# Two routed feed-forward passes and a recurrence on one core: another order for the router's front, the weights and the scatters

## The reference

```python
x = L0_attn_h
x = x + 0.5 * ffn(layernorm(x))          # first pass
x = x + recurrence(layernorm(x))         # 3 layers of width 64, a scan over each sequence
x = x + 0.5 * ffn(layernorm(x))          # second pass

def ffn(x):                              # 8 experts, the best one of each token
    p = softmax(x @ Wr + br); gate = max(p); e = argmax(p)
    xn = layernorm(x) * ln_g + ln_b
    return (relu(xn @ W1[e] + b1[e]) @ W2[e] + b2[e]) * gate
```

## Time and profile before

| | us |
|---|---|
| median of 3 runs | 731.2 |
| lowest and highest | 726.25, 731.56 |
| the profiled execution | 730.1 |
| its span in the trace | 728.4 |
| PE busy | 667.5 (92%) |
| DVE busy | 409.2 (56%) |
| ACT busy | 270.0 (37%) |
| POOL busy | 173.6 (24%) |

### The profile page before, as it was taken

How to read it: one execution, slowest core, us unless ns; L and a number is a source line. 1 busy time by engine, 2 the same in 40 slices (tenths; PEclk the granted TensorE clock), 3 DMA queues, 4 the chain that set the end, 5 groups by cost and what they waited for, 6 DMA issues and landing times.

```text
span 728.4 us, 15522 instructions
## 1 busy us (share of the span) xinstructions
PE 667.5 (92%) x4414; PEld 583.2 (80%) x4414; DVE 409.2 (56%) x1427; ACT 270.0 (37%) x640; POOL 173.6 (24%) x178
## 2 busy tenths in 40 slices
PE   5567998899999999999998999999899989999993
PEld 4346997699997987888867877878789979999992
DVE  7256676233345667686888677787756533333331
ACT  3222321132325467553553556744422313222220
POOL 4611533211112111113412241123304411111111
PEclk9997999899999999999999999999989999999998
DMA  9929893675654454434615417343274564553540
GB/s 289 288 95 320 270 313 118 232 241 170 205 208 139 154 194 139 146 109 142 234 53 186 145 55 278 133 130 119 68 262 150 200 207 162 189 161 123 168 141 14
DMA packets 59919, 126.51 MB, mean 174 GB/s; under 512 B 8105, under 2 KB 36660, under 8 KB 59700
## 3 DMA queue, kind: packets, MB, share of 16 engines
q1 hardware_dynamic: 53204, 108.50, 44.6%
q0 software_dynamic: 6624, 16.92, 6.4%
HBM read 106.36 MB, written 20.35 MB: 174 GB/s over the span
## 4 chain that ended last, share of the span: by engine, by line
PE 64%; DVE 15%; issue 8%; DVEq 6%; another core or an unknown queue 2%; DMA 2%; ACT 1%; POOL 0%; SPq 0%; POOLq 0%; ACTq 0%
PE bank L1670 27%; PE bank L1684 27%; PE bank L1657 2%; DMA pay<-routed_rows 2%; DVEq L397 2%; DVE st L735 1%; PE bank L1516 1%; PE bank L1578 1%; DVE rec L1070 1%; DVE y_b L1169 1%; DVE act_t L1160 1%; PE bank L1611 1%; PE bank L1585 1%; DVE rec L1046 1%
## 5 line engine op out<-in xcount | busy, mean ns | idle before, releaser
L1670 PE MATMUL bank<-mn_t,w 128*128 128x128 f32 x2368 | 287.0, 278 | 0.1
L1670 PEld LDWEIGHTS bank<-mn_t,w 128*128 128x128 f32 x2368 | 277.4, 194 | 8.2 <-issue 8.0
L1684 PE MATMUL bank<-w,act_t 128*128 x1184 | 277.6, 385 | 5.7 <-DVE res L1175 4.0
L1684 PEld LDWEIGHTS bank<-w,act_t 128*128 128x128 f32 x1184 | 220.2, 192 | 43.5 <-issue 16.7
L1397 ACT ACTIVATE mn_t<-bank,vec 128x128 f32<-128x128 f32 x152 | 61.4, 454 | 228.9 <-PE bank L1657 208.4
L1160 DVE TENSOR_SCALAR act_t<-bank,vec 128x128 f32<-128x128 f32 x296 | 83.4, 344 | 109.1 <-PE bank L1670 94.8
L1407 ACT ACTIVATE act_t<-bank,vec 128x128 f32<-128x128 f32 x296 | 84.7, 368 | 78.0 <-PE bank L1670 75.9
L1169 DVE TENSOR_TENSOR y_b<-bank,b_all 128x256 f32<-128x256 f32 x74 | 31.4, 425 | 110.1 <-PE bank L1684 95.4
L634 POOL DMA_INDIRECT out_x<-res,pay x37 | 37.4, 1011 | 210.5 <-DVE res L1175 131.0
L634 POOL DMA_INDIRECT x_middle<-res,pay x37 | 37.0, 999 | 212.3 <-DVE res L1175 177.6
L625 POOL DMA_INDIRECT routed_rows<-rows,dest x64 | 65.7, 1027 | 64.5 <-DVE dest L840 32.4
(11 more groups left out here) (213 smaller groups left out, 462.2 us busy)
## 6 DMA issues: line engine op xcount, KB each, us to landing
w<-in_L_ffn_W SPq DMA_DIRECT2D x82, 1024.0 KB, 8.7
pay<-routed_rows SPq DMA_DIRECT2D x78, 130.0 KB, 2.1
rows<-in_L_attn_h SPq DMA_DIRECT2D x8, 512.0 KB, 5.5
rows<-x_middle SPq DMA_DIRECT2D x8, 512.0 KB, 4.5
routed_rows<-fill SPq DMA_DIRECT2D x2, 1040.0 KB
routed_rows<-rows,dest POOLq DMA_INDIRECT x64
b_all<-in_L_ffn_b SPq DMA_DIRECT2D x1, 1024.0 KB, 9.0
x_middle<-res,pay POOLq DMA_INDIRECT x37, 2.7
```

The lines of the kernel that those rows point to most:

```text
L1670: last = t.matmul(b_hid[half][:, c % 4 * P:(c % 4 + 1) * P], w1[i % W1S][:, k * F + c * P:k * F + (c + 1) * P], mn_t[p][i % 2][:, k * P:(k ...
L1684: last = t.matmul(b_out[i % 2], act_t[i % 2][:, c * P:(c + 1) * P], w2[:, ds(eb * (WE // FC) + c * D, D)], start=c == 0, stop=c == FC - 1)
```

## The change

- **Constants.** POOL makes the identity first and raises `s_c1` to 1; tri and the counters follow (2), the rest last (3). PE starts at 1, DVE's copies at 2.
- **PE.** It begins with seven unread products (`in_motion(7)`), and waits for `s_c2` only ahead of `router_sums`. Chunk 1's transposes and logits now stand ahead of chunk 0's ranks; `parameters` ahead of chunk 2's turned logits. Chunk 3's transposes, logits and turned logits leave the front for columns 0, 48, 192 and 216, which are slots 0 and 1. ACT's copies follow.
- **DVE.** choose 0, place 0, choose 1, copy of count 0, place 1, copy of count 1. `order_of_use` is gone.
- **POOL.** It issues four scatters, then waits until both counts are copied, then issues twelve.
- **SP.** Chunk 0, router weights, chunk 1, router bias, chunk 2, four second weights, parameters, the other four second weights, chunk 3; after the tables the first weights of slot 0, the rows of slots 0 to 3, the first weights of slot 1, output bias, first weights of slot 2. No weights by use; the first second product waits for all eight.
- **Columns.** The parameters' columns and the log of the sigmoid move from slot 6 (312 of 48 each) to slot 1 (72). Chunk 3 of the recurrence and of the second router moves back by up to some two slots, chunks 0 to 2 hardly.

```diff
-LN_MOMENTS = [[984, 985], [1272, 1273], [1680, 1681], [2064, 2066]]
+LN_MOMENTS = [[984, 985], [1272, 1273], [1680, 1683], [2064, 2113]]
...
-UP = [[5760, 5856], [7057, 7104], [9480, 9504], [10584, 10944]]
+UP = [[5760, 5856], [7057, 7104], [9528, 9600], [11112, 11184]]
...
-CONVOLVE = [[1033, 1300, 1752, 2136], [1176, 1442, 2040, 2352], [1298, 1657, 2256, 2497]]
-GATES = [[4248, 5328, 7056, 8640], [4800, 5832, 8256, 9481], [5208, 6720, 9120, 10176]]
+CONVOLVE = [[1033, 1300, 1752, 2211], [1176, 1442, 2040, 2378], [1298, 1656, 2256, 2616]]
+GATES = [[4248, 5328, 7056, 9048], [4800, 5832, 8256, 9552], [5232, 6721, 9144, 10560]]
...
-R_RANKS = [[None, None, 192, 552], [6240, 7944, 9816, 11280]]
+R_RANKS = [[None, None, 193, 552], [6240, 7944, 9936, 11472]]
...
+R1_TRANSPOSE = [0, 48]
+R1_KEEP = [0, 24]
+R1_LOGITS = 192
+R1_KEEP_LOGITS = 49
+R_TURN_LOGITS = [[None, None, None, 216], [5952, 7368, 9696, 11256]]
 R_SCATTER = [[[None, None, None, None], [None, None, None, None], [72, 120, 168, 216], [264, 312, 360, 408]],
-    [[1560, 1608, 1656, 1704], [2040, 2088, 2136, 2160], [2472, 2520, 2568, 2616], [2808, 2856, 2904, 2952]]]
+    [[1560, 1608, 1656, 1704], [2040, 2088, 2136, 2160], [2472, 2520, 2568, 2616], [2856, 2904, 2952, 3000]]]
...
-LAYER_COLUMNS = 96
-EXP_LOG_A = 120
-LOG_SIGMOID = 312
+LAYER_COLUMNS = 49
+EXP_LOG_A = 72
+LOG_SIGMOID = 72
...
             sp.dma_start(rb_all[:, :], router_b[None, :].to_broadcast([P, E])).then_inc(s_rb, 16)
-            for e in range(EAGER):
+            load_x(0, 2)
+            for e in range(E // 2):
                 second_weights(e)
-            load_x(0, 2)
+            load_parameters()
+            for e in range(E // 2, E):
+                second_weights(e)
             load_x(0, 3)
-            load_parameters()
 
             sp.wait_ge(s_tab, 1)
-            for i in range(2):
-                slot_weights(0, i)
-            sp.wait_ge(s_order, 1)
-            second_weights_by_use(0)
+            slot_weights(0, 0)
             for i in range(RING - 1):
                 next_rows(0, i)
-            second_weights_by_use(1)
+            slot_weights(0, 1)
...
             g.memset(ident[:, :], 0.0)
+            pool.drain()
+            g.affine_select(out=ident[:, :], in_=ident[:, :], compare_op=ALU.not_equal, fill=1.0, base=0,
+                            pattern=[[-1, P]], channel_multiplier=1).then_inc(s_c1, 1)
...
                 for part in range(NJ // 2):
+                    if (c, part) == (0, 2):
+
+                        pool.wait_ge(s_kept[R1], HC)
                     route(0, c, part)
...
-            for c in range(HC):
-                choose(0, c)
-                place(0, c)
-                keep_counts(0, c)
+            choose(0, 0)
+            place(0, 0)
+            choose(0, 1)
+            keep_counts(0, 0)
+            place(0, 1)
+            keep_counts(0, 1)
             for part in range(5):
                 tables(0, 0, part)
-            order_of_use()
...
             def second_expert(p, i):
-                if p == 0 and i < LATER:
-
-                    if i == 0:
-                        pe.wait_ge(s_w, 16 * EAGER)
-                    pe.wait_ge(s_wl[i], 16)
+                if (p, i) == (0, 0):
+                    pe.wait_ge(s_w, 16 * E)
                 return expert_of(pe, p, i)
...
-            pe.wait_ge(s_c2, 1)
+            pe.wait_ge(s_c1, 1)
+            in_motion(7)
             for part in range(2):
                 transposes(R1, 0, part)
+            pe.wait_ge(s_c2, 1)
             router_sums()
             pe.wait_ge(s_wrk, 1)
             logits(R1, 0)
+            transposes(R1, 1, 0)
             turn_logits(0, 0)
-            transposes(R1, 1, 0)
-            ranks(0, 0)
             transposes(R1, 1, 1)
             logits(R1, 1)
+            ranks(0, 0)
             turn_logits(0, 1)
             counts(0, 0)
+            ranks(0, 1)
             transposes(R1, 2, 0)
-            ranks(0, 1)
+            counts(0, 1)
             transposes(R1, 2, 1)
-            counts(0, 1)
             logits(R1, 2)
+            parameters()
             turn_logits(0, 2)
-            for part in range(2):
-                transposes(R1, 3, part)
-            logits(R1, 3)
-            parameters()
-            turn_logits(0, 3)
             pe.wait_ge(s_tpe, 2)
             pe.wait_ge(s_tab, 1)
             in_motion(8)
```

More of the change, by code:

```diff
@@ L588, in _ @@
             g.iota(iota_i[:, ENTRIES + 2 * E:ENTRIES + 2 * E + 1], [[0, 1]], base=0, channel_multiplier=1)
-            g.iota(iota_i[:, ENTRIES + 2 * E + 1:ENTRIES + 2 * E + 1 + LATER], [[FC, LATER]], base=EAGER * FC,
-                   channel_multiplier=0)
+            pool.drain()
+            g.affine_select(out=tri_f[:, :], in_=tri_f[:, :], compare_op=ALU.is_ge, fill=0.0, base=-1,
+                            pattern=[[1, P]], channel_multiplier=-1).then_inc(s_c1, 1)
             g.iota(rows_t[:, :, C_ID:C_ID + 1].bitcast(I32).rearrange("p t w -> p (t w)"), [[P, NT]], base=0,
@@ L605, in _ @@
             for b in range(NB):
-                g.memset(half_sel[b * DO:(b + 1) * DO, b:b + 1], 1.0)
                 pool.drain()
-            g.affine_select(out=ident[:, :], in_=ident[:, :], compare_op=ALU.not_equal, fill=1.0, base=0,
-                            pattern=[[-1, P]], channel_multiplier=1)
-            g.affine_select(out=tri_f[:, :], in_=tri_f[:, :], compare_op=ALU.is_ge, fill=0.0, base=-1,
-                            pattern=[[1, P]], channel_multiplier=-1).then_inc(s_c1, 1)
+                last = g.memset(half_sel[b * DO:(b + 1) * DO, b:b + 1], 1.0)
+            last.then_inc(s_c1, 1)
+            pool.drain()
             def powers(m, c):
@@ L720, in _ @@
             last.then_inc(s_c2, 1)
+            dve.wait_ge(s_c1, 3)
             def moments(m, c, part):
@@ L1373, in beside @@
                                 keep(LN, c, part)
+                            if c == NC - 1 and k == R1_KEEP[part]:
+                                keep(R1, c, part)
+                        if c == NC - 1 and k == R1_KEEP_LOGITS:
+                            keep_logits(R1, c)
                         if k == LN_KEEP_LOGITS[c]:
@@ L1460, in _ @@
             keep_logits(R1, 0)
-            keep(R1, 1, 0)
+            for part in range(2):
+                keep(R1, 1, part)
             exponentials(0, 0)
-            keep(R1, 1, 1)
             keep_logits(R1, 1)
+            exponentials(0, 1)
             keep(R1, 2, 0)
-            exponentials(0, 1)
             keep(R1, 2, 1)
             keep_logits(R1, 2)
-            for part in range(2):
-                keep(R1, 3, part)
-            keep_logits(R1, 3)
             parameters()
@@ L1623, in beside @@
                                 up(c, part)
+                            if c == NC - 1 and k == R1_TRANSPOSE[part]:
+                                transposes(R1, c, part)
+                        if c == NC - 1 and k == R1_LOGITS:
+                            logits(R1, c)
                         if k == LN_LOGITS[c]:
@@ L1637, in beside @@
                         for f in range(FFNS):
-                            if f and k == R_TURN_LOGITS[c]:
+                            if k == R_TURN_LOGITS[f][c]:
                                 turn_logits(f, c)
```

120 lines of the change are left out of this document (36 added, 84 removed).

## The result

The changed kernel took 724.09 us (median of 15 runs, 721.49 to 727.60), beside it the kernel before 731.29 (15 runs, 725.24 to 734.90): a ratio of 0.991, 95% interval 0.988 to 0.993. Its profiled execution took 724.11 us with a span of 722.4, against 730.1 and 728.4. The forecast was 724.1 for the median and 723.0 for the profile.

What follows compares the result with a forecast made beforehand. PE bounds the kernel from the first product on, so gains lie in the front and single PE gaps. Terms -6.6 + 3.7 - 1.1 + 0.5 - 3.6 = -7.1 us gave 723.0 profiled, 724.1 median; own range 718 to 729, overall 716 to 731.

Steps and rivals of the forecast that it cites:

- The start: Front: SP's load stream sets the start; slot 0's rows land at 55.4 us instead of 62.04, -6.6 us.
- The tables: Front: with count 1 early and twelve scatters behind both counts, the tables are ready by 36 us.
- rival (a): Front: PE is held by the scatters again; the start gains 3, sum -3.5, 727.7 us; chance 0.18.
- one of the prediction's own signs of being wrong: Front: an ACT or PE wait that ends with the last scatter.
- Chunk 3 in the slots: Slots 0 and 1: chunk 3's transposes, logits and turned logits move where PE is the bound, +3.7 us.
- The log: Log of the sigmoid: leaving slot 6 ends a PE gap, -1.1 us; in slot 1 it costs +0.5 us.
- Chunk 3's convolution and gates: Recurrence: moving them out of a stage's beginning saves a 2.57 us PE gap and low-clock time, -3.6 us.
- another of its signs of being wrong: Later slots: new PE gaps over 1 us from slot 40 on.
- Rival (c): Second pass: the last stage starves behind chunk 3's later scatters; three slots late gives +10.6, 734.7 us; chance 0.10.
- Rival (b): Front: early weights take what the scatters gave; rows at 62 again, start 0, sum -0.5, 730.7 us; chance 0.12.

Runs made afterwards that it cites:

- the third chip: Chip of a repeat: kernel before unchanged 729.44 us, changed kernel unchanged 722.38 us (ratio 0.987), and two second weights behind slot 1's weight with old columns 716.79 us.
- second chip: Chip where four variants of the changed kernel ran first (chunk 3's router in front, late log, old columns, parameters first): 723.80, 725.95, 721.79, 717.97 us.
- the last run: Kernel before with twelve of the sixteen scatters held until the first tables are ready, on a fourth chip: 729.22 us, ratio 1.000.

## Why the prediction was right, and where it was right by luck

**The start (-6.6).** Measured -6.30 (58.40), and -5.4 between the two traces of the third chip (64.05 and 58.63). The mechanism was the one forecast: SP's stream, 3 us a MB, rows in at 55.74 against 55.4. Moving 2 MB behind the rows moved them 6 us; taking away the stall (second chip), holding the scatters or leaving out the products at the start moved the first product by no more than 0.6. What is missing is a run of the kernel before with SP's new order alone.

**The tables (36).** This sentence failed: 42.7, although count 1 came at 23.58, ahead of the 26 to 28 of the forecast. The prediction took the late copy of count 1 for the whole stall, and thought that twelve scatters behind both counts have only slot work behind them. DVE's tables, ACT's copies and PE's logits stand beside them and waited as before, as rival (a) had it. It didn't show in the time because SP issued slot 0's weight 3.7 us later still (46.40). Rival (a)'s mechanism took place, without its price, and with it one of the prediction's own signs of being wrong: an ACT wait that lasts until after the last scatter (42.49).

**Chunk 3 in the slots (+3.7).** +3.29 to slot 5, 0.65 of it from the log, in the profiled pair. But slot 0 of the profiled kernel before ran at the low clock (5.99 us), and in the three other traces of that front it took 3.79; against those the changed kernel is 4.5 to 6.7 us longer up to slot 5. Its first slot met the 1.2 GHz level each time (granted clock 0.50), after a front in which PE had been busy 16 to 18 of the 39 us from 17 to 56 (six traces whose first product comes at 58 to 59), against 21 to 25 in the traces of before. The sum kept the clock's loss on both sides alike; that this fitted is the luck of the one profile of before. Up to slot 9, where much of it evens out, the forecast has +3.1 for chunk 3 and the log together, the pair shows +0.74 and the third chip's pair +1.35. What the move bought was not in the forecast: with chunk 3 in the front, the start didn't come early in either order that was tried (64.22 under the stall, 62.35 with its input loaded last).

**The log (-1.1 and +0.5).** -1.5 and +0.65. Slots 5 to 8 gained 2.55 in the pair and more against the other traces of before, where this stretch took 43.7 to 44.2. In those PE waits 1.89, 3.01 and 2.46 us at the place of the 1.09. So the term for slots 5 to 8 was mis-sized by 1 to 3 us; the log is 1.5 of it, and the rest is not isolated.

**Chunk 3's convolution and gates (-3.6).** The step that failed most: -0.48 in the pair, -0.5 in the middle of fourteen traces. The named gap did go, but PE waited 1.26 and 0.53 us beside it for other pieces, 1.43 us at the next stage's beginning, where another wait got shorter, and the low clock at the beginning of the stage stayed (5.34 us for sixteen products). New gaps over 1 us from slot 40 on were another of its signs of being wrong. With the columns of before the gap comes back (2.56 us at 431.04), and yet that trace has the shortest stretch of all. One gap was priced as if nothing would take its place.

**The sum** was -7.1 and is -5.98 in the profiles, -7.2 in the medians. The term for chunk 3's convolution and gates fell short by 3.1 us, the slots up to 9 came out 2.4 cheaper, and the two stood against each other. The start, which is most of the gain, was right by its mechanism; that the sum came so close was luck. Rival (c) did not come: the last stage begins with the same gap as before. Rival (b) neither.

**Which chip.** The waits marked "remote" were seen on three of the four chips of the experiments. On the other the kernel before takes 719.8 us, 11 us less. That this is the price of the stall in its front (its tables wait for a count that is held 12 us) is argued from four traces without the stall, and not from a trace of the kernel before on that chip, of which there is none. Against it stands that holding the scatters in the kernel before, tried twice, moved the stall and gained nothing in the time. The changed kernel's own time there wasn't measured; its relatives (721.8 with the old columns, 723.8 with chunk 3 in front, 726.0 with the late log) suggest that it is no faster there than the kernel before, perhaps a little slower. If so, the change makes the kernel indifferent to the stall rather than faster by itself. The version with two second weights behind the rows took 719.2 where the kernel before took 731.2, and with the old columns 716.8 where they took 731.5 (before) and 722.4 (changed).

## What to carry to other kernels

When a stall is removed by reordering, ask who works beside its cause in the new order: here the wait found a new victim each time, and the gain came from having a stream of loads that was longer than the stall. Price the bytes ahead of the first input of the main loop, since a MB moved behind it was worth its full 3 us here while the DMA engines were full. A single gap ahead of one piece of work is no price for moving that piece: take the distance between two fixed points over several traces, and its spread.

## What the runs showed of the hardware

- While POOL issued indirect scatters one every 1.28 us, engines that waited for other engines were released 3 to 12 us after the work that they waited for had ended: DVE at 42.14 for a count that PE ended at 30.27 (kernel before), ACT at 42.49 for products that ended at 33.06 (changed), at 55.34 for products that ended at 47.39 (the last run). DVE paused 0.4 to 3.1 us between small instructions. The last such release came 2.3 us after the start of the last scatter's issue in the kernel before, 3.9 in the changed one, and 3.2 in the last run, 0.15 us before SP went on behind the landed scatters (55.49). With the scatters held until the tables, the changed kernel shows none. What in the chip does this stays open.
- Of four chips one did not show it at all, with the same scatters at the same pace (four traces); there the kernel before was 1.6% faster. Whether the one is the cause of the other is not shown.
- The same instructions of slots 9 to 34 took 224.5 to 225.1 us in all fourteen traces, on all chips, and slots 58 to 73 105.26 in all but one: between such fixed points one trace is exact to a few tenths. Where stages begin it isn't (4 us).
